# Vision block with routed experts on one core: 120-column chunks at the end of each expert list, and transposes of the maxima that load twelve columns

## What is computed

```python
capacity = int(CAP_RATIO * N / E)            # 1.2 * 12608 / 8 = 1891
for k in range(TOP_K):                       # TOP_K = 2
    ...
    keep = posk < capacity
    buf = buf.at[ik, posk].set(jnp.arange(N, dtype=jnp.int32), mode='drop')
    xg = xpad[buf]
    h = jnp.einsum('ecd,edh->ech', xg, W1)
    act = h[..., :H] * jax.nn.silu(h[..., H:])
    ye = jnp.einsum('ech,ehd->ecd', act, W2)
    ...
    out = out.at[buf.reshape(-1)].add((w_buf[..., None] * ye).reshape(E * capacity, D), mode='drop')
```

## Time and profile before

| | us |
|---|---|
| median of 3 runs | 2298.15 (2297.8 to 2298.42) |
| the profiled execution | 2295.04 |
| its span, first to last instruction | 2293.3 |
| TensorE busy | 2099.6 (92%) |
| VectorE busy | 1596.9 (70%) |
| GpSimd busy | 1591.3 (69%) |
| ScalarE busy | 1082.8 (47%) |

### The profile page before, as it was taken

How to read it: one execution, slowest core, us unless ns; L and a number is a source line. 1 busy time by engine, 2 the same in 40 slices (tenths; PEclk the granted TensorE clock), 3 DMA queues, 4 the chain that set the end, 5 groups by cost and what they waited for, 6 DMA issues and landing times. The chain is left out here.

```text
span 2293.3 us, 48656 instructions
## 1 busy us (share of the span) xinstructions
PE 2099.6 (92%) x14580; PEld 2021.3 (88%) x14580; DVE 1596.9 (70%) x4319; ACT 1082.8 (47%) x2850; POOL 1591.3 (69%) x2317
## 2 busy tenths in 40 slices
PE   5999999999999999999999299999999999999980
PEld 4899999999999999999988299999999999999980
DVE  5578877777778777878787356665666666666657
ACT  2454444444444444444444145454544545454545
POOL 3466767676767676767666667777777777777766
PEclk8999999999999999999999599999999999999995
DMA  7656565656565656565643243201010101001338
GB/s 200 151 132 150 133 148 132 148 131 147 132 146 132 146 133 145 132 146 132 146 105 85 56 93 49 41 5 29 3 31 5 31 5 29 4 4 23 56 45 340
DMA packets 235842, 223.52 MB, mean 97 GB/s; under 512 B 90648, under 2 KB 216067, under 8 KB 234689
## 3 DMA queue, kind: packets, MB, share of 16 engines
q1 hardware_dynamic: 135872, 147.40, 25.5%
q10 hardware_dynamic: 45568, 59.31, 11.2%
q0 software_dynamic: 54272, 15.20, 5.4%
HBM read 154.56 MB, written 98.38 MB: 110 GB/s over the span
## 5 line engine op out<-in xcount | busy, mean ns | idle before, releaser
L1175 POOL DMA_INDIRECT x_tokens<-yout,e_entry x240 | 383.6, 1598 | 180.0 <-DVE yout L1356 133.7
L678 PE MATMUL Y<-p,vp 128*102 128x198 f32 x1536 | 360.0, 344 | 21.8 <-ACT ysb L491 19.3
L447 POOL DMA_INDIRECT expert_lists<-entry,slot x256 | 300.2, 1173 | 54.2 <-issue 54.2
L1371 DVE TENSOR_TENSOR a<-UP,gate 128x384 f32<-128x384 f32 x320 | 178.4, 558 | 218.2 <-ACT gate L1311 212.7
L1160 POOL DMA_INDIRECT rows<-x_wide,e_entry x240 | 249.5, 1039 | 79.1 <-issue 72.0
L1311 ACT ACTIVATE gate<-GT 128x384 f32<-128x384 f32 x320 | 157.4, 492 | 297.2 <-PE UP L1253 297.1
L496 ACT ACTIVATE p<-ST 128x396 f32<-128x396 f32 x384 | 190.7, 497 | 223.4 <-PE ST L650 218.7
L141 POOL TENSOR_TENSOR word_p<-word_p 1x1 f32<-1x1 f32 x416 | 93.2, 224 | 256.9 <-ACT p L498 244.3
L413 POOL TENSOR_TENSOR x_lo<-x,x_hi 128x396 fp32r<-128x396 f32 x192 | 205.6, 1073 | 76.8 <-ACT x_hi L467 72.9
L678 PEld LDWEIGHTS Y<-p,vp 128*102 128x102 f32 x1536 | 221.3, 170 | 36.5 <-POOL p L435 19.0
L854 DVE TENSOR_REDUCE rm<-S 128x2 f32<-128x256 f32 x384 | 161.7, 421 | 85.9 <-PE S L669 80.2
(11 more groups left out here) (220 smaller groups left out, 6540.8 us busy)
## 6 DMA issues: line engine op xcount, KB each, us to landing
x<-in_xt ACTq DMA_DIRECT2D x180, 198.0 KB
q<-qk_features SPq DMA_DIRECT2D x384, 74.2 KB
k<-qk_features SPq DMA_DIRECT2D x192, 148.5 KB
qk_features<-qk_hi SPq DMA_DIRECT2D x96, 198.0 KB, 2.9
qk_features<-qk_lo SPq DMA_DIRECT2D x96, 198.0 KB, 3.8
rb<-rd ACTq DMA_DIRECT2D x128, 74.2 KB
t_x<-x_tokens SPq DMA_DIRECT2D x15, 576.0 KB, 7.5
out<-t_o ACTq DMA_DIRECT2D x15, 576.0 KB, 7.3
```

Of the source, the lines that this page charges most:

```text
L447: pool.indirect_dma_start(d["lists"][:, :], bass.IndirectOffsetOnAxis(ap=slot[o][0:REAL[t], t, c:c + 1], axis=0), entry[o][0:REAL[t], t, c ...
L678: return pe.matmul(Y[0:VW1, 0:TI], v0, p32[b][:, hh, 0:TI], start=start, stop=stop)
L1175: pool.indirect_dma_start(d["x1"][:, :], row_of(cc, t), yout[q][:], None, bounds_check=N - 1, oob_is_err=False, compute_op=ALU.add)\
L1371: dve.tensor_tensor(a32[m % 2][:], UP[m % 2][:, 0:TILE3], gate[m % 2][:], ALU.mult)\
```

## The change

In the expert stage the last chunk of each list, every fifth of the 80, takes 120 slots a tile and not 128: `LAST` is the smallest even number with three tiles over 1891 - 1536 = 355, so 360 slots and not 384. The slots left out are above the capacity and never hold a token. `rows_of` gives the rows of a tile, `columns` cuts 3 x 120 columns out of 384. The gathers and scatters get 120 rows, the transposes 120 partitions and 120 columns of identity, `first` 360 moving columns, and `second` 120 weight columns and 120 result rows; what ScalarE and VectorE do between them goes over 3 x 120 columns or 120 partitions. In attention the two transposes of `rm` load its first 12 columns and write 12 rows. No instruction is added, left out or moved on any engine, and the waits are the same.

```diff
-                            pe.transpose(G[b][:, 0:P], rm[im][:, 0, :], ident[:])
-                            pe.transpose(G[b][:, P:TI], rm[im][0:T1, 1, :], ident[0:T1, 0:T1])\
+                            pe.transpose(G[b][0:NH, 0:P], rm[im][:, 0, 0:NH], ident[:])
+                            pe.transpose(G[b][0:NH, P:TI], rm[im][0:T1, 1, 0:NH], ident[0:T1, 0:T1])\
                                 .then_inc(full[b], 1)
...
+        LAST = -(-(CAP - (SEG - TILE3)) // 6) * 2
+
+        def rows_of(cc):
+
+            return LAST if cc % (CPE // K2) == CPE // K2 - 1 else P
+
+        def columns(ap, cc):
+
+            w = rows_of(cc)
+            ap = ap[:, 0:TILE3]
+            return ap if w == P else ap.rearrange("p (t c) -> p t c", t=3)[:, :, 0:w]
...
-                pool.indirect_dma_start(rows[cc % 2][:, t, :], None, d["xin"][:, :], row_of(cc, t),
+                pool.indirect_dma_start(rows[cc % 2][0:rows_of(cc), t, :], None, d["xin"][:, :], row_of(cc, t),
...
-                    d["x1"][:, :], row_of(cc, t), yout[q][:], None, bounds_check=N - 1, oob_is_err=False, compute_op=ALU.add)\
+                    d["x1"][:, :], row_of(cc, t), yout[q][0:rows_of(cc)], None, bounds_check=N - 1, oob_is_err=False, compute_op=ALU.add)\
...
-                        mm = pe.transpose(XT[b][:, t * P:(t + 1) * P], rows[cc % 2][:, t, b * P:(b + 1) * P],
-                                          ident[:])
+                        w = rows_of(cc)
+                        mm = pe.transpose(XT[b][:, t * P:t * P + w], rows[cc % 2][0:w, t, b * P:(b + 1) * P],
+                                          ident[0:w, 0:w])
...
-                        mm = pe.matmul(bank[:, 0:TILE3], a, b[:], start=(k == 0), stop=(k == 4))
+                        mm = pe.matmul(columns(bank, cc), a, columns(b, cc), start=(k == 0), stop=(k == 4))
...
-                c = slice(t * P, (t + 1) * P)
+                r = rows_of(cc)
+                c = slice(t * P, t * P + r)
...
-                    pe.matmul(y[:, 0:C], a_lo[q][:, m, c], w2[e][:, m, 0], start=False, stop=False)
+                    pe.matmul(y[0:r, 0:C], a_lo[q][:, m, c], w2[e][:, m, 0], start=False, stop=False)
...
-                    dve.tensor_tensor(a32[m % 2][:], UP[m % 2][:, 0:TILE3], gate[m % 2][:], ALU.mult)\
+                    dve.tensor_tensor(columns(a32[m % 2], cc), columns(UP[m % 2], cc), columns(gate[m % 2], cc),
+                                      ALU.mult)\
                         .then_inc(s_a, 1)
```

More of the change, by code:

```diff
@@ L1066, in expert_block @@
         s_out = [sem(f"y_scattered{n}") for n in range(6)]
+        LAST = -(-(CAP - (SEG - TILE3)) // 6) * 2
[5 more added lines that the diff above has]
+            return ap if w == P else ap.rearrange("p (t c) -> p t c", t=3)[:, :, 0:w]
         def weight_of(cc, t):
-            return entry[cc % NB][:, t, 0:1]
+            return entry[cc % NB][0:rows_of(cc), t, 0:1]
         def row_of(cc, t):
-            return bass.IndirectOffsetOnAxis(ap=entry[cc % NB][:, t, 1:2].bitcast(I32), axis=0)
+            return bass.IndirectOffsetOnAxis(ap=entry[cc % NB][0:rows_of(cc), t, 1:2].bitcast(I32), axis=0)
         last_x, last_o = ([sb(f"t_{name}_{n}", [P, LT, C], F32) for n in range(LB)] for name in ("x", "o"))
@@ L1265, in wide @@
                     def wide():
-                        return pe.matmul(y[:, 0:2 * C], a_hi[q][:, m, c],
+                        return pe.matmul(y[0:r, 0:2 * C], a_hi[q][:, m, c],
                                          w2[e][:, m].rearrange("p a b -> p (a b)"),
@@ L1292, in rows_hi @@
                 act.wait_ge(s_xt, cc + 1)
-                act.activation(x0_hi[cc % 2][:], XT[0][:, 0:TILE3], ACT.Copy).then_inc(s_xhi, 1)
-                act.activation(x1[cc % 2][:], XT[1][:, 0:TILE3], ACT.Copy).then_inc(s_xhi, 1)
+                act.activation(columns(x0_hi[cc % 2], cc), columns(XT[0], cc), ACT.Copy).then_inc(s_xhi, 1)
+                act.activation(columns(x1[cc % 2], cc), columns(XT[1], cc), ACT.Copy).then_inc(s_xhi, 1)
             def y_lo(cc, t):
@@ L1299, in y_lo @@
                 act.wait_ge(s_y, n + 1)
-                act.activation(ylo[n % 2][:], Y[n % 2][:, C:2 * C], ACT.Copy,
+                r = rows_of(cc)
+                act.activation(ylo[n % 2][0:r], Y[n % 2][0:r, C:2 * C], ACT.Copy,
                                scale=weight_of(cc, t)).then_inc(s_ylo, 1)
@@ L1304, in hidden_hi @@
                 act.wait_ge(s_a, 4 * cc + m + 1)
-                act.activation(a_hi[cc % 2][:, m], a32[m % 2][:], ACT.Copy).then_inc(s_ahi, 1)
+                act.activation(columns(a_hi[cc % 2][:, m], cc), columns(a32[m % 2], cc), ACT.Copy).then_inc(s_ahi, 1)
             rows_hi(0)
@@ L1310, in _ @@
                     act.wait_ge(s_ug, 4 * cc + m + 1)
-                    act.activation(gate[m % 2][:], GT[m % 2][:, 0:TILE3], ACT.Silu).then_inc(s_gate, 1)
+                    act.activation(columns(gate[m % 2], cc), columns(GT[m % 2], cc), ACT.Silu).then_inc(s_gate, 1)
                     if cc and m:
@@ L1346, in rows_lo @@
                 dve.wait_ge(s_xhi, 2 * cc + 2)
-                dve.tensor_tensor(x0_lo[q][:], XT[0][:, 0:TILE3], x0_hi[q][:].bitcast(F32), ALU.subtract)
-                dve.tensor_tensor(x1[q][C2:P, :], XT[1][C2:P, 0:TILE3], x1[q][C2:P, :].bitcast(F32),
-                                  ALU.subtract).then_inc(s_split, 1)
+                dve.tensor_tensor(columns(x0_lo[q], cc), columns(XT[0], cc), columns(x0_hi[q], cc).bitcast(F32),
+                                  ALU.subtract)
+                dve.tensor_tensor(columns(x1[q][C2:P], cc), columns(XT[1][C2:P], cc),
+                                  columns(x1[q][C2:P], cc).bitcast(F32), ALU.subtract).then_inc(s_split, 1)
             def y_out(cc, t):
@@ L1355, in y_out @@
                 wait(dve, s_out[q], 16 * (cc // 2))
-                dve.scalar_tensor_tensor(out=yout[q][:], in0=Y[n % 2][:, 0:C], scalar=weight_of(cc, t),
-                                         in1=ylo[n % 2][:], op0=ALU.mult, op1=ALU.add).then_inc(s_yout, 1)
+                r = rows_of(cc)
+                dve.scalar_tensor_tensor(out=yout[q][0:r], in0=Y[n % 2][0:r, 0:C], scalar=weight_of(cc, t),
+                                         in1=ylo[n % 2][0:r], op0=ALU.mult, op1=ALU.add).then_inc(s_yout, 1)
             def hidden_lo(cc, m):
                 dve.wait_ge(s_ahi, 4 * cc + m + 1)
-                dve.tensor_tensor(a_lo[cc % 2][:, m], a32[m % 2][:], a_hi[cc % 2][:, m].bitcast(F32),
-                                  ALU.subtract).then_inc(s_alo, 1)
+                dve.tensor_tensor(columns(a_lo[cc % 2][:, m], cc), columns(a32[m % 2], cc),
+                                  columns(a_hi[cc % 2][:, m], cc).bitcast(F32), ALU.subtract).then_inc(s_alo, 1)
             rows_lo(0)
```

## The result

The changed kernel takes 2291.67 us (median of 13 runs, 2287.02 to 2295.5). The kernel before, run beside it on the same chip, takes 2296.9 us (13 runs, 2291.01 to 2298.42). The ratio is 0.9981, 95% interval 0.9972 to 0.999: a gain of 4.4 us by the ratio, 5.2 by the medians, of the 9.2 that were forecast. The time lies in the predicted range (2285 to 2293), but not at the predicted 2289.0, and the gain is 0.19% by the ratio, 0.23% by the medians, just at the 0.2% that separates "faster" from "no change". The profiled execution took 2290.9 us, 2289.2 of it the span; before it was 2295.04 and 2293.3, and 2285.8 was forecast for it.

A forecast was written before the change was run, and what follows sets the result against it. The distance from one TensorE matmul to the next was taken to bound the kernel. Sixteen short chunks (8.9 us), stops (0.2) and tail (0.1) gave 9.2 us, taking 2298.15 to 2289.0, range 2285 to 2293.

The forecast's parts named there:

- First products: Expert stage, L1253: 40 matmuls of a short chunk stream 360 columns, not 384; 0.437 us saved a chunk, seams free.
- Second products and transposes: Expert stage, short chunks: 120-column weight loads save 0.08 us a chunk; turning the rows with 120 columns saves 0.04 us.
- The three terms: Expert stage, per short chunk: matmul columns 0.437, weight loads 0.08 and row transposes 0.04 us, together 0.56 us.
- The places: TensorE's 11.09 us loop: 10.65 in a short chunk, the one before 0.04 and the one after 0.08 us under 11.09.
- The stops: TensorE's seven waits at changes of expert: each at most 0.03 us shorter, 0.2 us in all, still 2.0 us long.
- The other engines: ScalarE, VectorE, GpSimd: less work worth nothing; GpSimd issues up to 0.2 us dearer each, 1.1 a short chunk, covered by waiting.
- The turned maxima: Attention, L734 and L735: 64 transpose pairs loading 12 columns gain 0, as loads were hidden; gain bound 3.2 us.
- Rival (A): Attention, L734 and L735: the 12-column load makes TensorE stop, up to 20.5 us lost, 2309.4 us; chance 0.07.
- The clock: Half-clock stretch after one stop of seven in the expert stage: zero or three move the time by -1.6 or +3.3 us.
- the small terms: Expert stage, short chunks: two small load terms, 0.08 us for second products and 0.04 us for turning rows, each possibly 0.
- The chances: Whole kernel: faster (under 2293.55 us) 0.86, same 0.09, slower 0.05; the forecast itself 0.80.

The follow-up runs named there:

- full transfers: Changed kernel with gathers and scatter-adds of the short chunks at all 128 rows again, engines' work still at 120: 2291.05 us in a single run.
- the chunks alone: Kernel before with only the 120-slot tiles in every fifth chunk, the transposes of the maxima left as before: 2291.99 us, ratio 0.9975.
- the first four experiments: Kernel before with only the 12-column transposes (1.0001) or only the 120-slot chunks (0.9975); before and changed kernels with VectorE's weight split earlier, removing stops (0.9912, 0.9883).

## Why the prediction was right or wrong

**First products.** Right. Predicted 0.437 us a short chunk and 0.164 us from matmul to matmul; measured 0.164. The seams between three pieces cost nothing at 120 columns, as put. The row used for it (L644) didn't show that this holds only for some widths: at 126 a seam would have eaten all.

**Second products and transposes.** Right in kind. Loads of 120 columns last 182 ns for most (predicted 182), a wide product behind a narrow one comes after 191 ns and not 196, and a transpose of a short chunk after 103 and not 109. Not foreseen: the first product after short transposes comes 184 ns behind and not 177. The three terms together were 0.56 us and measured 0.54 to 0.55.

**The places.** A short chunk and its neighbours share the gain otherwise than listed. From the transposes of one chunk to those of the next it is 10.83, 10.85 and 11.03 us around a short chunk, where it was 11.09, so that most of the sum falls into two distances and not one. The sum is as predicted.

**The stops.** Right: predicted 0.03 us less each, measured 0.04, and still 2.0 us long.

**The other engines.** Right for the path. GpSimd's issues rose by up to 0.37 us each on average, over the 0.2 that was put as the bound, but by 0.65 us a short chunk, within the 1.1; the wait for `yout` covered it, and full transfers gave no time back.

**The turned maxima.** Right: 0, with the loads at 88 ns. Rival (A) and the rule of the Trainium skill named beside it ("TensorEngine Tiling (Array Packing)", Key Properties: a change of tiling mode drains TensorE) don't show here. A load of 12 columns between loads of 102 and 128 left the distances as they were in the medians: 109 ns from the start of L734 to that of L735, 230 ns from the end of L735 to that of L644. Either it enters no such mode, or the change costs nothing visible; these runs don't tell which.

**The clock: the step that failed.** The prediction had seen one half-clock stretch behind one of seven stops and made of it a spread, "zero or three such stretches move the time by -1.6 or +3.3 us", around an unchanged middle. The size was right and the kind wrong. How many stops are followed by such a stretch depends on the distance between them, and the change alters just that: 1.0 to 1.1 us less from stop to stop. The runs show 5.4 +- 2.5 us more half-clock time on the average (162.1 against 156.7), which gives back up to 2.7 us, and 6.6 +- 2.2 us (up to 3.3) with the chunks alone. The 156.7 is of the runs beside the first four experiments, as no clock is on record for those beside the changed kernel itself. The loop of a short chunk saves 0.54 to 0.55 us in the traces, 8.7 us for sixteen; less 2.7 that is 6.0, with the 0.3 us of stops 6.3, beside 5.2 by the medians and 4.4 by the ratio. The ratio's interval is +-2.1 us, so that by these means most of the missing 4 to 4.8 us is the clock, 0.2 us or so the small terms, and the rest within the noise.

**Luck.** That the time fell into the range is in part luck. The forecast started from 2298.15, the median of three runs; the kernel before took 2296.9 beside the changed one. With that start the same gain would have forecast 2287.7, and the miss would have been 4.0 us and not 2.7.

**The chances.** 0.86 for faster by over 0.2% was too sure for a forecast of 0.4% whose bound, 2293.55, could be reached by three such stretches. The spread of the clock stood in the range and was left out of the chances. By the ratio of 0.9981 the gain did not reach the 0.2% at all.

**What stays open.** Why these distances and not others, and which single stop is followed by a stretch: a stretch moves the next stop by 1.56 us, so that one hit bears on the next, as the even pattern of the changed kernel shows, but the runs only give the half-clock time at five pairs of distances with stops of 2 us (111.7 to 112.0, and 113.7 to 114.1: high; 112.5 to 113.3: low); no law for it was measured. Nor is it shown what makes pieces of 126 and 124 columns dearer than those of 120.

## What to carry to other kernels

Where a profile has short stops of TensorE at even distances, with a half-clock stretch behind some of them, a change of the work between the stops also changes how many are hit. Price it as a term that can go either way (here up to 3.3 us given back on a gain of 9, and about 4 us lost with 1 us more between the stops), judge it by the mean granted clock of many runs and not by one profile, and look first whether the stops can go. Here moving one instruction of VectorE to an earlier place in its queue, which removed them, was worth 21.4 us on top of the change's 4 to 5, and 19.4 us on the kernel before. Reckon too with the start of the forecast: a median of three runs was off by 1.3 us here, as much as a seventh of the gain.

## What the hardware showed that was not expected

A stop of 1.99 us was enough to bring a stretch at a granted clock of 0.50, and then 1.56 us of loss; one of 0.57 us never did in 7. The same stop in the same place of the program brings it in some runs and not in others, and the distance between the stops moves how often: 1 us more or less moved the mean half-clock time from about 156 to 163 us in both directions.

A moving operand in three pieces costs a matmul nothing at 120 columns a piece (163.6 ns for 360), 1.7 ns at 124 and 2.8 ns at 126, where it takes the time of the full 384.

An indirect scatter-add of 120 rows takes GpSimd longer to issue than one of 128: 1.95 us on average for a short chunk's third, against 1.57 for the same one with 128 rows, and 0.05 us more for the first and second.
